# Attention sums of a graph network in two column groups of TensorE instead of four: one-hots beside 32 zero columns, `ps_acc` as four blocks of 64x384

## The reference

```python
ft = jnp.einsum('nhd,ed->nhe', hh, W_fc)
a1 = jnp.einsum('nhd,hd->nh', ft, attn_l)
a2 = jnp.einsum('nhd,hd->nh', ft, attn_r)
e = jax.nn.leaky_relu(a1[src] + a2[dst], negative_slope=NEG_SLOPE)
m = jax.ops.segment_max(e, dst, num_segments=n)
ee = jnp.exp(e - m[dst])
denom = jax.ops.segment_sum(ee, dst, num_segments=n)
alpha = ee / denom[dst]
agg = jax.ops.segment_sum(alpha[:, :, None] * ft[src], dst, num_segments=n)
res = jnp.einsum('nhd,ed->nhe', hh, W_res)
return jax.nn.relu((res + agg).reshape(n, H * D))
```

## Time and profile before

| | us |
|---|---|
| median of 3 runs | 1934.79 |
| lowest, highest | 1933.72, 1936.58 |
| span of the profiled execution | 2277.0 |
| PE busy in the span | 1621.1 (71%) |
| POOL busy | 1232.7 (54%) |
| DVE busy | 1121.9 (49%) |
| ACT busy | 718.1 (32%) |
| mean data rate in the span | 257 GB/s |

### The profile page before, as it was taken

One profiled execution on the slowest core, in us unless ns is written; L12 is line 12 of the kernel. 1 busy time (PEld: TensorE's weight loads), 2 busy tenths in 40 slices (PEclk: granted clock), 3 DMA queues, 4 the chain that ended last, 5 costly groups with the idle time before them and its releaser, 6 DMA issues. The chain is left out here.

```text
span 2277.0 us, 43588 instructions
## 1 busy us (share of the span) xinstructions
PE 1621.1 (71%) x13579; PEld 962.8 (42%) x13580; DVE 1121.9 (49%) x2027; ACT 718.1 (32%) x2184; POOL 1232.7 (54%) x1297
## 2 busy tenths in 40 slices
PE   7337888887778858787788887882666666666665
PEld 7223444444344424344444444671334444444443
DVE  6613334333334314444444444653666666666666
ACT  6400111111111101000000100262666666777675
POOL 2166566566656266566666666106555555555550
PEclk9969888899988869798988888986787777878877
DMA  4698888888878387788787887388788888888882
GB/s 183 218 315 269 268 266 271 274 265 277 275 264 270 125 279 270 261 270 277 262 274 266 266 275 274 122 310 280 245 279 267 270 267 272 273 273 272 273 276 84
DMA packets 139992, 585.22 MB, mean 257 GB/s; under 512 B 30616, under 2 KB 32752, under 8 KB 139946
## 3 DMA queue, kind: packets, MB, share of 16 engines
q0 software_dynamic: 100272, 497.49, 65.7%
q1 hardware_dynamic: 32563, 67.72, 8.6%
q10 hardware_dynamic: 7110, 19.43, 2.2%
HBM read 534.42 MB, written 50.12 MB: 257 GB/s over the span
## 5 line engine op out<-in xcount | busy, mean ns | idle before, releaser
L667 POOL DMA_INDIRECT ring_c<-table,slot_c x834 | 798.1, 957 | 545.9 <-issue 268.5
L1243 POOL DMA_INDIRECT ring<-table,slot x417 | 410.4, 984 | 288.5 <-issue 105.8
L833 DVE TENSOR_TENSOR hots<-iota,units 128x256 f32<-128x256 bf16 x102 | 43.3, 426 | 602.4 <-remote 332.9
L1493 PE MATMUL ps_acc<-ring,hot_f 128*32 128x195 f32 x3136 | 230.8, 386 | 138.2 <-issue 84.4
L1388 ACT ACTIVATE ring<-ring,weight x1152 | 281.5, 340 | 0.6
L1651 DVE TENSOR_TENSOR ring<-ring,ps_w 128x3120 f32 x72 | 244.7, 3398 | 16.5 <-issue 8.9
L1493 PEld LDWEIGHTS ps_acc<-ring,hot_f 128*32 128x32 f32 x3136 | 123.9, 125 | 227.7 <-issue 124.2
L808 PE MATMUL ps_ya<-weights,sum_ta 128*128 128x512 f32 (+1 forms) x576 | 204.1, 503 | 12.5 <-issue 10.9
L808 PE MATMUL ps_yb<-weights,sum_tb 128*128 128x512 f32 (+1 forms) x576 | 196.7, 494 | 6.1 <-issue 5.5
L711 ACT ACTIVATE slot_c<-units 128x8 int32 (+1 forms) x104 | 21.7, 211 | 545.9 <-DMA ring_c<-table,slot_c 391.8
L779 PE MATMUL ps_sum0b<-ring_c,hots 128*32 128x192 f32 x1600 | 136.3, 364 | 75.9 <-issue 66.6
(11 more groups left out here) (294 smaller groups left out, 2121.0 us busy)
## 6 DMA issues: line engine op xcount, KB each, us to landing
ring_c<-table,slot_c POOLq DMA_INDIRECT x834
table<-ft SPq DMA_DIRECT2D x25, 396.0 KB, 2.8
table<-nodes SPq DMA_DIRECT2D x25, 384.0 KB
table<-nodes ACTq DMA_DIRECT2D x25, 384.0 KB
turned_table<-h_t SPq DMA_DIRECT2D x25, 384.0 KB, 3.0
nodes<-in_x ACTq DMA_DIRECT2D x24, 384.0 KB
turned_g<-turned_table SPq DMA_DIRECT2D x24, 384.0 KB
out_x<-nodes SPq DMA_DIRECT2D x24, 384.0 KB
```

What stands on the lines that cost most here:

```text
L667: eng.indirect_dma_start(out=ring[:, t * QH + k, :], out_offset=None, in_=table, in_offset=bass.IndirectOffsetOnAxis(ap=slot[t][:, k:k + 1 ...
L833: eng.tensor_tensor(hots[k][:, :, :].rearrange("p (s c) d -> p s c d", c=CPU), iota0[:, :].unsqueeze(1).unsqueeze(2).to_broadcast([P, 2, C ...
L1243: eng.indirect_dma_start(out=ring[:, b * RB + at * FROW:b * RB + (at + 1) * FROW], out_offset=None, in_=table3, in_offset=bass.IndirectOff ...
L1493: last = eng.matmul(acc_of(s, g), hot_f[:, c, s * UD:(s + 1) * UD], ring[:, x0 + g * GW:x0 + (g + 1) * GW], start=False, stop=True, skip_g ...
```

## The change

The sums of the attention stage are laid out in two column groups of 64 instead of four of 32. Each group now takes six heads (390 columns). The one-hots of two neighbouring subtiles sit in one f32 block, with 32 zero columns between them (`hot_f[..., 3, UD]`, positions 0 and 2 filled, 1 left at zero): the 64 columns that begin at position 0 are the first subtile's one-hots and zeros, those that begin at position 1 are zeros and the second's. So each matmul adds to 64 partitions, of which 32 receive zeros. `ps_acc` has its head group in the upper or lower 64 partitions and the pair of subtiles in a bank. The shared slice has a copy without zeros (`hot_x`) and serves two subtiles in one matmul. `lay` becomes 4 copies of 64x384, `cast_hot` becomes three activations, and the zeros are set once at the start.

```diff
-HG = H // US
+GA = 2
+UA = US // GA
+AW = UA * UD
...
-            PR = H // US
+            PR = H // GA
...
-            hot_f = sb(st, "hot_f", [P, UC, P])
+            hot_f = sb(st, "hot_f", [P, GA, CPU, 3, UD])
+            hot_x = sb(st, "hot_x", [P, P])
...
-            def acc_of(s, g):
-                return ps_acc[g * UD:(g + 1) * UD, s * 256:s * 256 + GW]
-
-            def by_subtile(width):
-                return ps_acc[:, :].rearrange("p (s x) -> p s x", s=US)[:, :, 0:GW].rearrange("p s (r c) -> p s r c", c=FH)[:, :, :, 0:width]
+            def acc_of(t, g):
+                return ps_acc[g * AW:(g + 1) * AW, t * 512:t * 512 + GW]
+
+            def hot_of(s, c):
+                return hot_f[:, s // UA, c, s % UA:s % UA + 2, :].rearrange("p x d -> p (x d)")
+
+            def by_half(width):
+                return ps_acc[:, :].rearrange("p (t x) -> p t x", t=GA)[:, :, 0:GW].rearrange("p t (r c) -> p t r c", c=FH)[:, :, :, 0:width]
...
-                        eng.activation(hot_f[:, :, :].rearrange("p c e -> p (c e)"), hot[:, ds(par, 1), :, :].rearrange("p a c e -> p (a c e)"), ACT.Copy).then_inc(hot_cast, 1)
+                        given = hot[:, ds(par, 1), :, :]
+                        for t in range(GA):
+                            eng.activation(hot_f[:, t, :, 0:3:2, :], given[:, :, 0:CPU, t * AW:(t + 1) * AW].rearrange("p a c (s d) -> p (a c) s d", d=UD), ACT.Copy)
+                        eng.activation(hot_x[:, :], given[:, :, CPU, :].rearrange("p a e -> p (a e)"), ACT.Copy).then_inc(hot_cast, 1)
...
-                        for g in range(US):
-                            for s in range(US):
-                                c0 = g // 2 * 512 + g % 2 * GN
-                                last = eng.activation(ps_n[s * UD:(s + 1) * UD, c0:c0 + GN], o[g * UD:(g + 1) * UD, s, :], ACT.Copy)
+                        for g in range(GA):
+                            for t in range(GA):
+                                last = eng.activation(ps_n[t * AW:(t + 1) * AW, g * 512:g * 512 + GN], o[g * AW:(g + 1) * AW, t, :], ACT.Copy)
                         last.then_inc(o_laid, 1)
...
                                 for c in range(CPU):
                                     x0 = b * RB + (s * CPU + c) * FROW
-                                    for g in range(US):
-                                        last = eng.matmul(acc_of(s, g), hot_f[:, c, s * UD:(s + 1) * UD], ring[:, x0 + g * GW:x0 + (g + 1) * GW],
+                                    for g in range(GA):
+                                        last = eng.matmul(acc_of(s // UA, g), hot_of(s, c), ring[:, x0 + g * GW:x0 + (g + 1) * GW],
                                                           start=False, stop=True, skip_group_check=True)
...
-                                for s in range(nu):
-                                    for g in range(US):
-                                        last = eng.matmul(acc_of(s, g), hot_f[:, CPU, s * UD:(s + 1) * UD], ring[:, x0 + g * GW:x0 + (g + 1) * GW],
+                                for t in range(-(-nu // UA)):
+                                    for g in range(GA):
+                                        last = eng.matmul(acc_of(t, g), hot_x[:, t * AW:(t + 1) * AW], ring[:, x0 + g * GW:x0 + (g + 1) * GW],
                                                           start=False, stop=True, skip_group_check=True)
...
+                    eng.memset(hot_f[:, :, :, :, :], 0.0)
...
-                    for g in range(US):
-                        for s in range(LU):
-                            r, c0 = slice(s * UD, (s + 1) * UD), g // 2 * 512 + g % 2 * GN
-                            last = eng.tensor_tensor(ps_s[r, c0:c0 + GN], ps_s[r, c0:c0 + GN], o[g * UD:(g + 1) * UD, s, :], ALU.add)
+                    for g in range(GA):
+                        r, c0 = slice(0, LU * UD), g * 512
+                        last = eng.tensor_tensor(ps_s[r, c0:c0 + GN], ps_s[r, c0:c0 + GN], o[g * AW:g * AW + LU * UD, 0, :], ALU.add)
```

More of the change, by code:

```diff
@@ L1234, in _ @@
                     eng.wait_ge(g_mask, 1)
-                    for g in range(US):
-                        last = eng.affine_select(out=head_of[:, g, :, :], in_=head_of[:, g, :, :], compare_op=ALU.not_equal, fill=1.0, base=-g * PR,
-                                                 pattern=[[-H, US], [-1, PR]], channel_multiplier=1)
+                    for g in range(GA):
+                        for s in range(UA):
+                            last = eng.affine_select(out=head_of[:, g, s, :, :], in_=head_of[:, g, s, :, :], compare_op=ALU.not_equal, fill=1.0, base=-s * H - g * PR,
+                                                     pattern=[[-UA * H, GA], [-1, PR]], channel_multiplier=1)
                     last.then_inc(g_const, 1)
@@ L1433, in rescale @@
                         eng.sem_inc(passed, 1)
-                        for g in range(US):
-                            last = eng.matmul(ps_l[g * UD:(g + 1) * UD, 64:64 + US * PR], lift[:, :], head_of[:, g, :, :].rearrange("p s k -> p (s k)"), start=True, stop=True)
+                        for g in range(GA):
+                            for s in range(UA):
+                                r0 = g * AW + s * UD
+                                last = eng.matmul(ps_l[r0:r0 + UD, 64:64 + GA * PR], lift[:, :], head_of[:, g, s, :, :].rearrange("p t k -> p (t k)"), start=True, stop=True)
                         last.then_inc(r_all, 1)
@@ L1482, in visit @@
                                     eng.sem_inc(passed, 1)
-                                for s in range(0, US, 2):
-                                    eng.matmul(ps_acc[:, s * 256:s * 256 + 2], ident_b[:, :], nil[:, :], start=True, stop=True, skip_group_check=True)
+                                for t in range(GA):
+                                    eng.matmul(ps_acc[:, t * 512:t * 512 + 2], ident_b[:, :], nil[:, :], start=True, stop=True, skip_group_check=True)
                             with eng.Else():
@@ L1567, in divide @@
                         eng.wait_ge(used[units_of(j) - 1], q + 2)
-                        eng.tensor_scalar(rden[:, :, :], by_subtile(FH)[:, :, :, DH], 0.5, None, ALU.max).then_inc(o_den, 1)
+                        eng.tensor_scalar(rden[:, :, :], by_half(FH)[:, :, :, DH], 0.5, None, ALU.max).then_inc(o_den, 1)
                         eng.wait_ge(o_den, j * 2 + 1)
@@ L1573, in divide @@
                             eng.wait_ge(o_laid, j)
-                        eng.tensor_tensor(o[:, :, :].rearrange("p s (r c) -> p s r c", c=DH), by_subtile(DH), rden[:, :, :].unsqueeze(3).to_broadcast([P, US, PR, DH]), ALU.mult).then_inc(o_made, 1)
+                        eng.tensor_tensor(o[:, :, :].rearrange("p s (r c) -> p s r c", c=DH), by_half(DH), rden[:, :, :].unsqueeze(3).to_broadcast([P, GA, PR, DH]), ALU.mult).then_inc(o_made, 1)
                     def finish(j):
                         eng.wait_ge(o_nat, j + 1)
-                        halves = ps_n[:, :].rearrange("p (g x) -> p g x", g=2)[:, :, 0:2 * GN]
-                        mine = node(j).rearrange("p (g x) -> p g x", g=2)
+                        halves = ps_n[:, :].rearrange("p (g x) -> p g x", g=GA)[:, :, 0:GN]
+                        mine = node(j).rearrange("p (g x) -> p g x", g=GA)
                         eng.scalar_tensor_tensor(out=mine, in0=halves, scalar=0.0, in1=mine, op0=ALU.max, op1=ALU.add).then_inc(o_fin, 1)
```

24 lines of the change are left out of this document (12 added, 12 removed).

## The result

The changed kernel takes 1941.15 us (median of 20 runs, 1929.38 to 1952.65), the kernel before 1932.34 (20 runs, 1924.72 to 1937.67). The ratio is 1.004, with an interval of 1.0026 to 1.0054: about 7.7 us slower, 0.3 us a quad (the medians differ by 8.8; where this text gives a difference in us, it is the ratio's). I had forecast +18.6. The direction was right, the size less than half, and behind it stand errors of opposite sign.

What follows compares the result with a forecast made beforehand. Two nearly tied loops, A (21.9 us) and loop B (22.2 a quad), were taken to bound attention; 24 quads x 0.85 = +20.4, less 1.8 at the end, gave 1934.8 + 18.6 = 1953 us, range 1918 to 1984.

Steps and rivals of the forecast that it cites:

- the saving is spent: Attention quad: TensorE's unit 2, shared and unit 3 use up `lay`'s 3.3 us; the terms-to-scaling stretch goes from 11.6 to 11.75.
- Unit 0's growth: First unit of a quad takes 1.8 us more where it starts slow, 1.23 where it is fast.
- loop B: Path over two quads through unit 0, 17 gathers, landing, terms, `lay` and scaling: 44.5 us, 46.4 after where unit 0 starts slow.
- The two accounts: Timed run and profile kept apart: timed 18.6 us slower; profiled span 2140 to 2190 from 2277.0, as the stall mostly vanishes.
- Units: TensorE's sums, two groups of 64 columns running at once: 2.65 us in a train, about 2.8 with the end.
- The tail: TensorE behind `scores`: unit 2, shared and unit 3, 2.65 + 1.35 + 2.85 = 6.85 us.
- The casts: `cast_hot` in three pieces of 256, 256 and 128: 1.06 us, 0.32 more.
- The end: Adds at the end: eight at 2.95 us become two of 384 columns at about 1.1, saving 1.8.
- The clock: Unit 0 starts at the half level and the clock rises 3.4 to 3.8 us in: about 4.6 us.
- unit 0 stays fast: Rival, chance 0.10: the clock never falls ahead of unit 0, which takes 2.65 us; 1914 us if A decides.
- A: Path of the last full quad, unit 0 to the next unit 0, through `lay` and scaling: 21.9 us before, 22.0 after.
- The signs: Expected in the trace: `divide` waiting for unit 3, last full quad 21.5 to 22.5, no 1.2 us "issue" gaps, span under 2200.

Runs made afterwards that it cites:

- short `lay`: Kernel before with six of `lay`'s sixteen copies, part of the output missing: 1912.25 us, ratio 0.9908; 0.9992 where the kernel before takes 2286.98.
- before again: The kernel before, unchanged, run for a second trace: 1932.28 us, ratio 1.0007.
- early signal: VectorE releases `sloped` behind the last use of the previous scores; on the kernel before 0.9999, 1.0005, 0.9999 and 1.0004, only where that takes 2287 to 2314 us.

## Why the prediction was right or wrong

**The step that failed** is "the saving is spent". I put the pass from the terms to the scaling at 0.5 + 11.6 before and 0.5 + 11.75 after. The second was nearly right: 12.41 in the pass shown. The first was 2.1 us short: 14.25. The missing part is `sloped` (1.85 us) and 0.3 behind `lay`. The earlier trace rows have it 0.03 us after `scores`, because in the last full quad the terms are taken early and the scaling of unit 2 is past by then; in each of the other quads it waits for VectorE's queue. So shortening `lay` by 3.38 had 1.6 to 1.8 us to give, where the forecast took +0.15. I read the path of the gather-bound quads from the one quad that isn't gather-bound. The 12.25 after also has a holder that I had not named, VectorE's chain from `sloped` to the scores, which ends with TensorE's tail.

**Unit 0's growth** was too large as well: 1.8 and 1.23 us, 1.55 in the mean, for +0.94 measured (2.55 to 3.49 over the 25 first units).

**The term that was missing** has the other sign: the wait at unit 2's place, +0.65 us a quad. I had placed the cost of slower units in unit 0 alone and left loop C out, which goes over one quad: unit 2 used, nine gathers (unit 2's four, the shared one, unit 3's four), the landing, the terms, the scaling of unit 2, unit 2 again. The rows from 1604.24 to 1629.31 are one round of it, 25.07 us: terms and scaling 3.7, unit 2 4.43, 0.83 from its recorded end to the gather, 12.2 for nine gathers (11.25 and 0.97 for a slow one), 3.9 until the terms have landed. With no slow gather that is 24.1, as long as the quad of 23.92 itself, and with a unit 2 of 2.84 it is 22.5.

+0.65 x 24 is 15.6; the wait for unit 0 gave 0.48 x 24 = 11.5 back. Of the +0.65, the short `lay` by itself brings 0.35 (the table). A rough estimate from these terms, whose closeness may be chance: loop B (-1.6 + 0.94)/2 = -0.33 a quad, and with loop C's +0.65 it is +0.3, for +0.27 in the trace and +0.85 in the forecast. That loop C is what holds the quad back is read from these rows; no run changed it alone at 1932 us.

**The two accounts** were half right. A timed run of the first kind doesn't have the 342 us, as I said, but not because recording costs them: the kernel before again was recorded at 1929.6. The expected span of 2140 to 2190 from a vanishing stall is refuted twice: 1927.6 where there is no stall, and 2279.3 where there is one and 88 matmuls a quad fewer did not lessen it. My bound of 24.9 us for the timed quad held (23.65), as did the price of the gathers in the layers:

```profile
L669 POOL DMA_INDIRECT ring_c<-table,slot_c x834: 942/946/1900, 111.9 to 1199.7; - x167
```

That is 1088 us from the first of 834 gathers to the last, against 1323.6 in the earlier trace rows (112.2 to 1435.8), and near the floor of 834 x 1.25 = 1042.

**Units**: expected 2.65 in a train and 2.8 with the end, measured 2.79 and 2.84. One after the other they would have been 5.2, so two groups of 64 columns do run at once. The Trainium skill, TensorEngine Tiling (Array Packing), "Tiling Modes", has them as independent tiles; the trace agrees, with 2.84 us for a unit. **The tail** 6.85, measured 6.8. **`lay`** 2.05, measured 1.98. **The casts** +0.32: 0.72 + 0.29 against 0.74, +0.27. **The end** -1.8: 2.95 to 1.13, the same.

**The clock.** I expected first units of 4.6 us (my own rise at 3.4 to 3.8 us gives 4.35 to 4.55). Of the 25, 13 take 2.84 us, all at the full level, eight take 4.29 to 5.14 and the rest lie between; before again, 19 of 25 had the 2.83 of the half level. The change holds the level more (0.81 to 0.94 in the same stretch). The last full quad was to stay at 22.0 and fell to 20.64, for unit 0 at 1883.75 took 2.84 and not 4.6. That is the rival "unit 0 stays fast", right about half of the first units and the quad without gathers, not about the sum, because loop B and loop C and not A set the others. It had also been my sign that the forecast's working fails.

**The signs.** `divide` no longer waits for `lay`, as expected, but the last full quad was to stay at 21.5 to 22.5. The span under 2200 and the absence of "issue" gaps prove nothing, since the old kernel has both at this speed. The 0.50 for the forecast's own range, 1940 to 1963, came true at its lower edge by terms that were wrong in both directions; that is luck.

## What to carry to other kernels

Take the path of a steady loop from a steady pass, not from the last one, where an order by hand has slack that the others don't have; then read, for each place in a ring of buffers, who frees it, since a faster stage on one place can be paid for at the next. A profile whose span is far from the timed runs needs a second one before any of its waits is explained: here the bound drawn from the difference held, and the explanation did not. And cut a copy only after asking what is late next: the short `lay` alone is worth 17.8 us, but the longer units of the layout that makes it short cost 25.5.

## What the runs showed of the hardware

The same kernel takes 1932 us on one chip and 2287 to 2314 on five others, at a mean granted clock of 0.875 against 0.82 to 0.83, with waits on TensorE that end up to 10 us after its recorded ends. Each of these chips has one batch of runs, so whether it is the chip or the hour is not shown. There, 16 more short matmuls a quad (32 recorded instructions) in unit 0 alone cost 36 us, while `lay`, 17.8 us at 1932, is worth nothing.

A granted clock that rises is no gain by itself: the change has 0.94 for 0.81 in the same 500 us and is slower. And units of 64 recorded instructions of 195 columns in four groups take 13.7 us more of the launch than units of 16 of 390 in two, with `lay` short in both: not in the steady quads (23.96 and 23.98 us) but by TensorE's next work starting up to 7.5 us behind VectorE's score after such a burst, in the first of them.

No kernel that does all of the work and clearly beats the kernel before was found; the change with the early signal was at 0.9976 in one batch and 1.0025 in the other. The short `lay` shows that 17.8 us lie there for a layout that needs fewer copies with units of the old length; the early signal at 1932 us is untried.
